# First gate of a two-layer graph and expert network: tokens normalized and picked four groups behind the mix instead of six, and freed PSUM banks used in the drain

## The reference

```python
x = x + _L0_gnn_ref(_layernorm(x), adj, W1, b1, W2, b2)
#   U = eigenvectors of the normalized Laplacian of adj (64 x 64)
#   agg = U.T @ features;  h = relu(agg @ W1 + b1);  back = U @ (h @ W2 + b2)
x = x + _L0_ffn_ref(_layernorm(x), Wg, bg, W1, b1, W2, b2)
#   gate_logits = xf @ Wg + bg                       (8 experts)
#   top_w, top_i = top_k(gate_logits, 2);  w = softmax(top_w)
#   out = sum over the two experts of w * (gelu(xf @ W1[e] + b1[e]) @ W2[e] + b2[e])
x = x + _L1_gnn_ref(...)      # two mixes over the graph, then LSTMs over windows of 2, 3 and 4
x = x + _L1_ffn_ref(...)      # dense up product, one expert of eight per token
```

## Time and profile before

| what | value |
|---|---|
| median of 3 runs | 1464.8 us (1462.32 to 1465.9) |
| profiled execution | 1469.62 us, of which the span of the instructions is 1467.9 us |
| mean granted TensorE clock | 0.892 |
| PE busy | 1120.2 us, 76% |
| DVE busy | 839.6 us, 57% |
| ACT busy | 749.9 us, 51% |
| POOL busy | 557.5 us, 38% |

### The profile page before, as it was taken

How to read it: one execution, slowest core, us unless ns; L and a number is a source line. 1 busy time by engine, 2 the same in 40 slices (tenths; PEclk the granted TensorE clock), 3 DMA queues, 4 the chain that set the end, 5 groups by cost and what they waited for, 6 DMA issues and landing times. The chain is left out here.

```text
span 1467.9 us, 28039 instructions
## 1 busy us (share of the span) xinstructions
PE 1120.2 (76%) x6333; PEld 829.7 (57%) x6334; DVE 839.6 (57%) x3907; ACT 749.9 (51%) x2074; POOL 557.5 (38%) x855
## 2 busy tenths in 40 slices
PE   2444422638862899999976998999999689929995
PEld 1223322527752799999974664445544345429995
DVE  4777798986775333344548993444444568622221
ACT  3555543623440566666644775665555466505552
POOL 3666614710367773045427710000000006644553
PEclk9999965568865899999997999999999899959998
DMA  9500000000012333233322200000000002243330
GB/s 257 136 1 1 1 1 0 1 1 5 24 44 65 101 122 94 69 103 103 103 69 51 53 8 1 0 0 0 0 1 0 4 1 85 87 130 102 105 103 26
DMA packets 85702, 75.57 MB, mean 51 GB/s; under 512 B 13207, under 2 KB 74848, under 8 KB 85613
## 3 DMA queue, kind: packets, MB, share of 16 engines
q1 hardware_dynamic: 71788, 44.64, 11.0%
q0 software_dynamic: 13824, 29.98, 6.5%
HBM read 41.72 MB, written 33.37 MB: 51 GB/s over the span
## 5 line engine op out<-in xcount | busy, mean ns | idle before, releaser
L1207 POOL DMA_INDIRECT z<-spent,seats x64 | 63.0, 985 | 393.4 <-DVE spent L1328 375.7
L1673 ACT ACTIVATE c_H<-ps,c_b 128x128 f32<-128x128 f32 x576 | 156.9, 383 | 98.4 <-PE ps L1719 98.4
L2234 PE MATMUL ps<-BIG,spent 128*128 x364 | 157.2, 581 | 3.4 <-ACTq L2247 3.4
L1719 PE MATMUL ps<-ZS,c_w 128*128 128x128 f32 x1152 | 143.3, 278 | 3.5 <-ACT ZS L1662 2.4
L1705 PE MATMUL ps<-spent,c_H 128*128 x1152 | 141.1, 276 | 0.0
L1719 PEld LDWEIGHTS ps<-ZS,c_w 128*128 128x128 f32 x1152 | 136.6, 195 | 4.6 <-ACT ZS L1662 3.0
L1705 PEld LDWEIGHTS ps<-spent,c_H 128*128 128x128 f32 x1152 | 135.2, 193 | 0.0
L2234 PEld LDWEIGHTS ps<-BIG,spent 128*128 128x128 f32 x364 | 70.1, 193 | 85.4 <-issue 85.4
L2242 PE MATMUL ps<-e_hs,spent 128*128 128x512 f32 (+1 forms) x256 | 110.0, 572 | 0.0
L856 POOL DMA_INDIRECT z<-BIG,spots x64 | 63.3, 990 | 113.3 <-DVE spots L973 95.9
L1573 POOL DMA_INDIRECT c_rows<-y,seats x64 | 60.4, 944 | 116.9 <-DMA y<-c_ys 62.2
(11 more groups left out here) (511 smaller groups left out, 2658.0 us busy)
## 6 DMA issues: line engine op xcount, KB each, us to landing
BIG<-z SPq DMA_DIRECT2D x72, 129.0 KB
ZB<-z SPq DMA_DIRECT2D x144, 64.0 KB
y<-c_ys SPq DMA_DIRECT2D x72, 128.0 KB
spent<-in_L_ffn_W_dram SPq DMA_DIRECT2D x1, 2048.0 KB
spent<-in_L_ffn_W_dram SPq DMA_DIRECT2D x8, 256.0 KB
w_dn<-in_L_ffn_Wd_dram SPq DMA_DIRECT2D x8, 256.0 KB
z<-BIG,spots POOLq DMA_INDIRECT x128, 2.2
z<-j_padding SPq DMA_DIRECT2D x9, 129.0 KB, 3.0
```

What stands on the lines that cost most here:

```text
L1207: pool.indirect_dma_start(z, bass.IndirectOffsetOnAxis(ap=k.seats[:, 0, n:n + 1], axis=0), k.R[:, row(n), :], None, bounds_check=E * STRID ...
L1673: act.activation(H[u][:, c, h * P:(h + 1) * P], UP[u][c // 2][:, o:o + P], ACT.Gelu, bias=b1[u][h][:, c:c + 1]).then_inc(gelu, 1)
L1719: pe.matmul(UP[u][c // 2][:, o:o + P], w1[u][h][:, c * P:(c + 1) * P], ZT[u][:, h * P:(h + 1) * P], start=True, stop=True).then_inc(up, 1)
L2234: last = pe.matmul(view(k.ps[4 * u + j], wide, lanes), k.w_ihT[:, w, :], state(i, u, s, p, wide, lanes), start=True, stop=(s == 0))
```

## The change

`LAG` becomes 4 in place of 6, and the two places of DVE's and PE's loops where the pick, the seat and the rank were written with fixed numbers now follow it. Normalizing, transposing, scoring, picking, ranking and seating all move two turns ahead, and the loops are two turns shorter. The mix, down and back products, `root_of`, `stats` and `spread` keep their turns. In the drain, ranks go to bank 0, odd groups' scores to bank 1 and odd groups' transposes to bank 2, and the waits that came from sharing a bank are loosened there.

```diff
-LAG = 6
+LAG = 4
@@ gate0_parts
-    RANK, COUNT = GA[:, GC // 2:GC // 2 + PAIR * PICKS * E], TR[:, 0:PICKS * E]
+    COUNT = TR[:, 0:PICKS * E]
+    FREED = GROUPS + 1
+
+    def rank_of(q):
+        bank = MIX[0] if 2 * q + LAG + 5 >= FREED else GA
+        return bank[:, GC // 2:GC // 2 + PAIR * PICKS * E]
+
+    def logits_of(n):
+        return MIX[1] if n % 2 and n + LAG + 2 >= FREED else GA
+
+    def turned_of(n):
+        return DN[0] if n % 2 and n + LAG + 1 >= FREED else TR
@@ add_gate_bias, seat and the copy of the transposes read logits_of(g), rank_of(q), turned_of(n)
@@ gate_vector
-            q_scale, q_pick, q_seat = (g - 3) // 2, (g - 9) // 2, (g - 10) // 2
+            q_scale, q_pick, q_seat = (g - 3) // 2, (g - LAG - 3) // 2, (g - LAG - 4) // 2
@@ rank
+            RANK, shared = rank_of(q), 2 * q + LAG + 5 < FREED
             pe.wait_ge(marked, q + 1)
-            pe.wait_ge(logits_sb, min(2 * q + 3, GROUPS))
+            if shared:
+                pe.wait_ge(logits_sb, min(2 * q + 3, GROUPS))
+            elif q:
+                pe.wait_ge(rank_read, q)
@@ gate_tensor
-            ranks = g % 2 and 0 <= (g - 11) // 2 < PAIRS
+            q_rank = (g - LAG - 5) // 2
+            ranks = g % 2 and 0 <= q_rank < PAIRS
...
                 pe.wait_ge(turned_sb, n + 1)
+                apart = g > FREED
                 if n >= 1:
-                    pe.wait_ge(logits_sb, n)
-                if ranks:
-                    pe.wait_ge(rank_read, (g - 11) // 2 + 1)
+                    pe.wait_ge(logits_sb, n - 1 if apart else n)
+                if ranks and g < FREED:
+                    pe.wait_ge(rank_read, q_rank + 1)
...
                 if n >= 1:
-                    pe.wait_ge(turned_sb, n)
+                    pe.wait_ge(turned_sb, n - 1 if g > FREED else n)
```

More of the change, by code:

```diff
@@ L927, in add_gate_bias @@
             dve.wait_ge(logits, g + 1)
-            tt_(group_of(k.LG, g), GA[:, 0:GT * E].rearrange("p (t e) -> p t e", e=E),
+            tt_(group_of(k.LG, g), logits_of(g)[:, 0:GT * E].rearrange("p (t e) -> p t e", e=E),
                 k.b_gate0[:, None, :].to_broadcast([P, GT, E]), ALU.add).then_inc(logits_sb, 1)
@@ L965, in seat @@
             dve.wait_ge(ranked, q + 1)
-            tt_(prod[:, :, :, :], RANK.rearrange("p (t c e) -> p t c e", c=PICKS, e=E),
+            tt_(prod[:, :, :, :], rank_of(q).rearrange("p (t c e) -> p t c e", c=PICKS, e=E),
                 k.chosen[:, tiles_of(q), :, :], ALU.mult).then_inc(rank_read, 1)
@@ L1080, in gate_scalar @@
                     act.wait_ge(logits, n - 1)
-                act.activation(k.ZS[n % 2][:, :], TR[:, :], ACT.Copy).then_inc(turned_sb, 1)
+                act.activation(k.ZS[n % 2][:, :], turned_of(n)[:, :], ACT.Copy).then_inc(turned_sb, 1)
         act.wait_ge(s_ex, 1)
@@ L1123, in gate_tensor @@
             if ranks:
-                rank((g - 11) // 2)
+                rank(q_rank)
             if LAG + 2 <= g <= GROUPS + LAG + 1:
@@ L1127, in gate_tensor @@
                 pe.wait_ge(turned_sb, n + 1)
+                apart = g > FREED
                 if n >= 1:
-                    pe.wait_ge(logits_sb, n)
-                if ranks:
-                    pe.wait_ge(rank_read, (g - 11) // 2 + 1)
+                    pe.wait_ge(logits_sb, n - 1 if apart else n)
+                if ranks and g < FREED:
+                    pe.wait_ge(rank_read, q_rank + 1)
                 for j in range(GT):
-                    last = pe.matmul(GA[:, j * E:(j + 1) * E], k.ZS[n % 2][:, j * P:(j + 1) * P],
+                    last = pe.matmul(logits_of(n)[:, j * E:(j + 1) * E], k.ZS[n % 2][:, j * P:(j + 1) * P],
                                      k.w_gate0[:, :], start=True, stop=True)
@@ L1139, in gate_tensor @@
                 if n >= 1:
-                    pe.wait_ge(turned_sb, n)
+                    pe.wait_ge(turned_sb, n - 1 if g > FREED else n)
                 for j in range(GT):
-                    last = pe.transpose(TR[:, j * P:(j + 1) * P], z_of(n * GT + j), k.ident[:, :])
+                    last = pe.transpose(turned_of(n)[:, j * P:(j + 1) * P], z_of(n * GT + j), k.ident[:, :])
                 last.then_inc(turned, 1)
```

## The result

The changed kernel takes 1504.17 us (median of 4 runs, 1501.45 to 1506.14) where the kernel before takes 1465.35 on the same occasions: 1.0268 times as long, 95% interval 1.0247 to 1.0288. That is 39 us; 38.3 were forecast, as 1503.

The account below looks back on a forecast made before the run. The prediction took the stage as bound by rank(3), plus a seat, plus 40 scatters on POOL. A first fetch 38.3 us later, with banks counted 0, added to 1464.8 gave 1503; 8-in-10 range 1488 to 1513.

Parts of the forecast that it names:

- What bounds the stage: POOL's gate scatters, starved for DVE's seats until ranks come, set the experts' first fetch; its shift enters the total one to one.
- the sign of some 10 us or more: On ACT, a wait of some 10 us or more for L924 before every even normalization would show the forecast true.
- The wait order on ACT: ACT's normalization waits for DVE's same-turn root_of, holding the copy that PE's scores need: +4.8 us per rank turn.
- The price: Chain on PE from seat's product through mean, normalization and ACT's copy to scores: 5.27 us instead of 0.44.
- The cycle: Rank to next rank in the mixing turns: 20.0 us at half clock, where it was 15.0.
- Which clock: PE runs the piece behind each rank at half clock after idling, which gives 1503; full clock would give 1485.
- The second case of the prediction: Rival: same stalls but PE keeps full clock, 18.2 us less, 1485 us; chance 0.13.
- three pieces of 3.4 and one of 2.6: Full-clock savings on PE: 3.4 us each behind scores (1) and ranks 0 to 2, 2.6 behind rank(3).
- The early turns and the end: Stalls ahead put rank(0) at 386.8 instead of 377.93; rank(6) at 490.1, first fetch 515.8 against 477.50, +38.3 us.
- The freed banks: Drain's ranks, scores and transposes in other banks: counted as 0, at most 1.3 us on rank(7).
- The fifth interval: In the drain, rank(4) to rank(5), still followed by root_of: 10.07 us becomes 13.3.
- The faster rival: Lead is won: each rank two turns earlier at present spacing, 14.1 us gained, 1451 us; chance 0.04.

Follow-up runs that it names:

- e5_wait_at_lag6: Changed kernel at LAG 6 with freed banks, ACT's normalization waiting for the same turn's root_of: 1503.01 us, 1.0256 times the kernel before.
- e3_copy_first: Changed kernel, but in each turn ACT copies the transposes out before it normalizes: 1484.18 us, 1.0128 times the kernel before.
- e6_warm: Changed kernel with six extra unread PE products behind each of ranks 0 to 3: 1492.08 us, 1.0198 times the kernel before.
- e2_lag_only: Changed kernel at LAG 4 with the freed banks never used (FREED = 99): 1505.94 us, 1.0284 times the kernel before.

## Why the prediction was right

*What bounds the stage.* Right: the shift of the first fetch, 39.3, is the loss of 39, and over all the kernels here that differ measurably the times stand in the order of their first fetches. ACT's waits before the even normalizations are 7.67, 9.98, four of 13.0, 12.02 and 6.50, so the sign of some 10 us or more holds for six of eight, not before every one.

*The wait order on ACT.* Right, and shown: by the chain in the three timelines, by `e5_wait_at_lag6`, which makes the loss with the wait alone, and by `e3_copy_first`, which moves the stall to the next instruction that needs ACT. The price was 5.27 from product to scores; it is 5.26 (413.75 - 408.49).

*The cycle.* 20.0 forecast, 20.48 measured. Two parts were off, by about the same: rank to seat's product, an estimate of 0.9, measured 1.11, and scores to add_bias, taken as 7.49 from the earlier trace rows, measured 7.74 (DVE's add_bias started at 421.49, the scores at 413.75). In the row scores and down product ran partly at full clock: they took 1.57 and 1.42 from their start to the next product's (379.08 to 380.65, 384.95 to 386.37), now 1.73 and 1.51. The last part, add_bias to the next rank, is 6.37 as forecast.

*Which clock.* Right that the piece behind each rank runs at half clock: the granted clock was 0.50 from 411 to 419 (columns as in the earlier trace rows), after PE had idled 2.47 and 5.29 us with only the small rank products between:

```profile
411.00:415.00 4.00, 1.25 (x6) 1.25 (x7) 1.24 (x7) 3.44 (x9) 3.09 (x4) 0.50 0.14 49
415.00:419.00 4.00, 4.00 (x17) 3.48 (x18) 0.19 (x1) 2.10 (x5) 3.08 (x4) 0.50 0.14 49
```

`e6_warm` puts the price at 3.6 us a pair; 3.4 was worked out. The second case of the prediction, 1485, would have asked for full clock in the early turns as well; with it behind the ranks alone it is 1492. By the prediction's own terms (three pieces of 3.4 and one of 2.6) the fetch would then come at 503.0; it came at 502.16.

*The early turns and the end.* rank(0) 386.8 forecast, 386.90 measured; rank(4) 465.1 and 466.35; rank(6) 490.1 and 490.64; last pair of scatters 493.1 and 493.42; fetch 515.8 and 516.78. These hits are closer than the working earned, since small errors cancel. Ahead of rank(0) the transposes started at 357.10 in place of 357.9, and the down product behind them took 1.67 in place of 0.9. After it the first three intervals were forecast 0.5 short each, the fourth 0.3 and the fifth 1.0 long (13.3 against 12.31), and the way from the last pair's first scatter to the fetch 0.6 short.

*The freed banks.* This term was mis-sized. It was counted as 0, with at most 1.3 us on rank(7). Counted from rank(3), so that the start of each execution drops out, they give 1.9 us by rank(6), which POOL waits for, and 2.5 by rank(7). The forecast held that the rank's wait for the scores' reading lies under the new chain; instead rank(4) waits 2.25 us for it without the banks, and with them 1.26 for the pick. The fifth interval, forecast without any help of the banks at 13.3, is 13.24 in `e2_lag_only`. The size is too small to show in the times, and the last ranks as they stand (496.62 and 497.73) hide it, because that execution's first rank was 0.84 earlier. At LAG 6 the banks are worth 4.4 on the last rank and 1.0 on rank(3).

*The faster rival.* It was right that the lead is worth something only if no wait takes its place. Whether it would have been 14 us could not be seen, since no run had LAG 4 without a stall. The runs that moved the lag without one speak for less: from LAG 8 to 6 and to 5, with the same banks, the first fetch goes 479.80, 475.78, 474.30.

## What to carry to other kernels

Where engines work through unrolled turns in fixed order, the distance between a producer's turn and its consumer's is what keeps a queue from blocking: before you shorten it, write down for each wait of the moved step in which turn its producer runs, and what is queued behind it. Here one wait that became due in its own turn cost 39 us, and no instruction was added. The loss sets in at once, not gradually (the ratios of LAG 8, 6 and 5 lie between 0.9998 and 1.0010, LAG 4 is 2.7% slower), although ACT's own wait of 5.80 us at LAG 5 announces it. The only gain found, 0.2%, was in the order of reading, picking and ranking at a distance that still had slack.

## What was not expected of the hardware

Extra work made a kernel faster, which the expectation of `e6_warm` had and the prediction had not considered. Six products whose result nobody reads, put into a wait of 5 us behind each of four ranks, made the changed kernel 10 to 12 us faster (by the ratios, 1.0268 and 1.0198, and by the medians, 1504.17 and 1492.08), because the granted clock over 410 to 453 rose from 0.66 to 0.90. This agrees with the Trainium skill (TensorE: Matmul & The Clock Gate, "What's actually happening"), by which activity is what releases the throttle.
